# A convolution and expert kernel on one Trainium2 core: the second stage with batched scales, statistics collected for the choice, and square roots by Newton steps on VectorE

## The reference

```python
z = layernorm(_ln_c(x), ln_w, ln_b)
ab = sigmoid(z @ gate_w + gate_b) * (z @ lin_w + lin_b) * z_mask
g = sigmoid(z @ eg_w + eg_b)
B = einsum('bikc,bkjc->bijc', protein_pair, ab) + einsum('bikc,bjkc->bijc', ab, compound_pair)
x1 = x + g * (layernorm(B, lnc_w, lnc_b) @ as_w + as_b) * z_mask
t = _ln_t(x1)                      # 16384 tokens of 128
probs = softmax(t @ Wr + br)       # 8 experts, the best two, weights that sum to 1
h = gelu(layernorm(t) @ W1[e] + b1[e]);  y = h @ W2[e] + b2[e]
out = x1 + w_a * y_a + w_b * y_b
```

## Time and profile before

| | us |
|---|---|
| median of 3 runs (989.59 to 992.62) | 990.55 |
| the profiled execution | 992.77 |
| its span, first to last instruction | 990.9 |
| busy: TensorE | 752.3 |
| busy: VectorE | 634.3 |
| busy: ScalarE | 603.4 |
| busy: GpSimd | 583.5 |
| blocks of half 0 | 119 to 159 |
| second stage of half 0, first statistics to last x1 | 159 to 239 |
| choice of half 0 | 247 to 269 |
| second stage of half 1 | 304 to 404 |
| GpSimd's 128 row transfers | 269 to 487 |
| tiles of the experts | 493 to 991 |

### The profile page before, as it was taken

The page is one execution under the profiler, slowest core; times in us unless marked ns, Lnnn a source line. Parts: engine busy times, 40 slices in busy tenths (PEclk is TensorE's granted clock), DMA queues, the critical chain, the costliest instruction groups (busy, mean ns, idle before and its releaser), DMA issues.

```text
span 990.9 us, 24898 instructions
## 1 busy us (share of the span) xinstructions
PE 752.3 (76%) x7186; PEld 657.3 (66%) x7187; DVE 634.3 (64%) x2187; ACT 603.4 (61%) x1247; POOL 583.5 (59%) x547
## 2 busy tenths in 40 slices
PE   2788895667594674358098989989939989899893
PEld 1677794556493463312088879888938988898793
DVE  5766404996704898562187878878826767667572
ACT  1868895564594554401086768777817867777681
POOL 4545101543177886887545766767754767767674
PEclk9989997798797687755588999999989999999897
DMA  9993305474013246441133443434324434434420
GB/s 255 329 326 113 92 1 170 146 218 146 5 57 128 90 138 202 135 150 68 55 96 106 133 125 106 127 111 137 103 65 128 128 108 137 128 99 128 120 86 19
DMA packets 124019, 124.21 MB, mean 125 GB/s; under 512 B 21886, under 2 KB 91415, under 8 KB 123963
## 3 DMA queue, kind: packets, MB, share of 16 engines
q1 hardware_dynamic: 90212, 80.24, 28.5%
q0 software_dynamic: 15296, 34.64, 10.1%
q10 hardware_dynamic: 18456, 8.67, 3.1%
HBM read 77.21 MB, written 48.68 MB: 127 GB/s over the span
## 4 chain that ended last, share of the span: by engine, by line
PE 57%; POOL 14%; DVE 12%; issue 10%; ACT 3%; DMA 2%; SPq 1%; DVEq 0%; ACTq 0%; POOLq 0%
POOL row_dram L475 7%; PE ps L1219 6%; PE ps L1220 6%; PE ps L1221 6%; PE ps L1239 6%; PE ps L1242 6%; PE ps L1240 6%; PE ps L1081 6%; POOL row_dram L464 4%; PE ps L1198 4%; PE ps L1132 3%; POOL rs L454 2%; PE ps L1233 2%; DVE stats L888 1%; DVE work L949 1%
## 5 line engine op out<-in xcount | busy, mean ns | idle before, releaser
L1038 DVE TENSOR_TENSOR rows<-ABz,rows 128x512 f16<-128x512 f32 x280 | 193.9, 693 | 93.6 <-ACT rows L691 91.4
L513 POOL DMA_INDIRECT row_dram<-PPb x140 | 160.2, 1144 | 89.3 <-DVE PPb L1047 49.0
L516 POOL DMA_INDIRECT out<-PPb x140 | 160.6, 1147 | 84.6 <-DVE PPb L1047 45.3
L690 ACT ACTIVATE ABz<-ps 128x512 f32<-128x512 f32 x280 | 169.0, 603 | 54.5 <-PE ps L1221 46.4
L1239 PE MATMUL ps<-PPb,rows 128*128 x1120 | 187.9, 222 | 0.0
L1240 PE MATMUL ps<-PPb,rows 128*128 x1120 | 187.7, 221 | 0.0
L691 ACT ACTIVATE rows<-ps 128x512 f16<-128x512 f32 x280 | 170.0, 607 | 0.0
L1219 PE MATMUL ps<-B,PPb 128*128 128x256 f16 x560 | 157.2, 281 | 4.2 <-issue 4.2
L1220 PE MATMUL ps<-B,PPb 128*128 128x256 f16 x560 | 157.2, 281 | 0.0
L1221 PE MATMUL ps<-B,PPb 128*128 128x256 f16 x560 | 157.1, 281 | 0.0
L1242 PE MATMUL ps<-PPb,rows 128*128 x1120 | 155.7, 221 | 0.0
(11 more groups left out here) (233 smaller groups left out, 1549.7 us busy)
## 6 DMA issues: line engine op xcount, KB each, us to landing
PPb<-row_dram SPq DMA_DIRECT2D x70, 264.0 KB, 2.8
PPb<-in_L_conv_protein_pair SPq DMA_DIRECT2D x32, 512.0 KB, 6.2
PPb<-row_dram SPq DMA_DIRECT2D x70, 136.0 KB, 2.6
rows<-in_x SPq DMA_DIRECT2D x32, 256.0 KB, 6.3
g_dram<-work ACTq DMA_DIRECT2D x32, 256.0 KB, 2.4
work<-g_dram SPq DMA_DIRECT2D x32, 256.0 KB, 2.8
ABT<-in_x SPq DMA_DIRECT2D x32, 256.0 KB, 3.0
row_dram<-PPb POOLq DMA_INDIRECT x140
```

The lines of the kernel that those rows point to most:

```text
L513: pool.indirect_dma_start(row2_dram, bass.IndirectOffsetOnAxis(ap=Rw[:, u, b, POS:POS + 1].bitcast(u32), axis=0), Rw[:, u, b, :], None, bo ...
L516: pool.indirect_dma_start(out_rows, bass.IndirectOffsetOnAxis(ap=Rw[:, u, b, TOK:TOK + 1].bitcast(u32), axis=0), Rw[:, u, b, 0:D], None, b ...
L690: act.activation(Hf[:, u % 2, q, :], full, ACT.Gelu, scale=1.0 / SCALE)
L1038: dve.tensor_tensor(rest[:, part], Hf[:, u % 2, q, :], high[:, part], ALU.subtract).then_inc(h_parts[q], 1)
```

## The change

The second stage is written in another way; what is computed stays the same.

- The scales of B are made in two batches for a half, for columns 0 to 15 and for 16 to 63, by VectorE alone (`scale_b`): the reciprocal square root is a shift and a subtraction on the bits (`MAGIC`) and three Newton steps. ScalarE's `norm_b` reads them from one table, `bsc`.
- For x1, only the statistics are taken in a group's step; all that follows them is done in `choose`, for the whole batch, in 16 more links of its chain (`STATS`), with the same Newton steps.
- VectorE writes x1 straight to `rows`; ScalarE's copy L637 is gone, and the gate buffers are free once x1 is written. In half 1 the writing waits for `moved`.
- GpSimd has no power in this stage: it moves ten groups, sets some buffers, moves six more, and scatters.
- `ranks(0)` and `weights(0)` are moved behind the first blocks of half 1, which then no longer wait for the choice of half 0 but for the first link of it; `SPLIT` is 32.
- SyncE loads the experts' weights in the middle of half 1 instead of behind it. Four of eight folds on TensorE come before the tables' product.
- All loops of the stage are unrolled.

```diff
-SPLIT = 28
+HEAD = 4
+SPLIT = 32
 BATCHES = ((0, 0, NC), (1, 0, SPLIT), (1, SPLIT, NC))
-AHEAD = 7
+AHEAD = 10
+MAGIC = float(0x5F3759DF)
...
+        bsc = sb("bsc", [P, 2, NC])
...
+        STATS = 16
+        TAIL, FSTEPS = STATS + 23, 16
...
-                    wait_reuse(sp, s.x1_kept, n, 4, GH * h)
-                    wait_reuse(sp, s.x1T_psum, n, 4, GH * h)
+                    wait_reuse(sp, s.x1_done, n, 4, GH * h)
...
+                for n in range(GH):
+                    load_gates(n, n % 4)
                     if h == 0:
                         pp_piece(1, n)
-                pipeline(sp, GH, 4, [(0, load_gates), (0, next_half)], depth=4)
-            sp.dma_start(W1s, W1.rearrange("e d h -> d e h")).then_inc(fw_loaded, 16)
-            sp.dma_start(W2s, W2.rearrange("e (k p) d -> p e k d", p=P)).then_inc(fw_loaded, 16)
-            sp.dma_start(b1r, b1.rearrange("(o e) d -> o (e d)", o=1)).then_inc(fw_loaded, 16)
-            sp.dma_start(gbn[0:NE, :], ffn_g).then_inc(fw_loaded, 16)
-            sp.dma_start(gbn[NE:, :], ffn_b).then_inc(fw_loaded, 16)
-            sp.dma_start(b2s, b2.rearrange("(o e) d -> o (e d)", o=1)).then_inc(fw_loaded, 16)
+                    if h == 1 and n == GH // 2:
+                        sp.dma_start(W1s, W1.rearrange("e d h -> d e h")).then_inc(fw_loaded, 16)
...
-                    pipeline(pool, GH, 2, [((0, X1LAG), power)])
-                    pool.wait_ge(s.tail, 12)
+                    pool.wait_ge(s.tail, 1)
...
-                    for i in range(STEPS):
-                        power(i, i % 2, [i < GH, i >= X1LAG])
-                        if i % 2 == 0 and AHEAD + i // 2 < GH:
-                            move_rows(AHEAD + i // 2)
-                        if i == GH:
-                            pool.wait_ge(s.tail_done, 2)
-                        if i >= GH:
-                            scatter(TG * (i - GH), TG * (i - GH + 1))
-                    scatter(TG * X1LAG, SPLIT)
+                    for g in range(AHEAD, GH):
+                        move_rows(g)
+                    pool.wait_ge(s.tail_done, 2)
+                    scatter(0, SPLIT)
...
+                if h:
+                    act.wait_ge(s.tail, 1)
...
+                        if h and q == 10:
+                            weights(0)
...
+                def norm_b(n):
+                    act.wait_ge(s.b_ready, 2 * h + (1 if n < HEAD else 2))
+                    wait_reuse(act, s.bT_psum, n, 2, g0)
                     for t in range(TG):
-                        i = act.activation(zh[:, w, 0:2, :].rearrange("p a e -> p (a e)")[:, t * C:(t + 1) * C],
-                                           B[:, bass.ds(n * TG + t, 1), :].rearrange("p a c -> p (a c)"), ACT.Identity,
-                                           bias=shift2[:, w, t:t + 1], scale=rsm2[:, w, t:t + 1])
+                        j = n * TG + t
+                        i = act.activation(bh[:, n % 2, t * C:(t + 1) * C], B[:, j, :], ACT.Identity, bias=bsc[:, 1, j:j + 1], scale=bsc[:, 0, j:j + 1])
...
-                    act.activation(rows[:, bass.ds(n * TG, TG), 0:D], gr[:, u, :, :], ACT.Copy).then_inc(s.x1_kept, 1)
...
+                for t in range(GH + 6):
+                    if t < GH:
+                        norm_b(t)
+                    if 0 <= t - 1 < GH:
+                        bT_copy(t - 1)
+                    if 0 <= t - 4 < GH:
+                        x1T_copy(t - 4)
+                    if 0 <= t - 6:
+                        logit_copy(t - 6)
+                    if h and t == SPLIT // TG + 6:
+                        weights(1)
...
+                dve.wait_ge(s.x1_stat, GH * h + j1 // TG)
+                sc = c.stat[:, 0:3 * nj].rearrange("p (v j) -> p v j", v=3)
+                v, y, hv, sq = (c.stat[:, a * nj:(a + 2) * nj].rearrange("p (v j) -> p v j", v=2) for a in (3, 5, 7, 9))
+                st = x1st[:, j0:j1, :]
+                dve.tensor_tensor(sc[:, 0, :], st[:, :, 1], st[:, :, 4], ALU.add)
+                dve.tensor_tensor(sc[:, 1, :], st[:, :, 1], st[:, :, 4], ALU.subtract)
+                tail(dve.tensor_tensor(sc[:, 2, :], st[:, :, 2], st[:, :, 5], ALU.add))
+                dve.tensor_scalar(sc[:, 0, :], sc[:, 0, :], -0.5, None, ALU.mult)
+                tail(dve.tensor_tensor(sc[:, 1, :], sc[:, 1, :], sc[:, 1, :], ALU.mult))
+                tail(dve.scalar_tensor_tensor(sc[:, 2, :], sc[:, 1, :], D / 4.0, sc[:, 2, :], ALU.mult, ALU.add))
+                dve.tensor_scalar(v[:, 0, :], sc[:, 2, :], 1.0 / D, 1e-5, ALU.mult, ALU.add)
+                tail(dve.tensor_scalar(v[:, 1, :], sc[:, 2, :], (1.0 + 1e-5) / D, 1e-10, ALU.mult, ALU.add))
+                dve.tensor_scalar(hv, v, -0.5, None, ALU.mult)
+                tail(dve.tensor_scalar(y.bitcast(i32), v.bitcast(i32), 1, None, ALU.arith_shift_right))
+                tail(dve.tensor_scalar(y.bitcast(i32), y.bitcast(i32), -1.0, MAGIC, ALU.mult, ALU.add))
+                for _ in range(3):
+                    tail(dve.tensor_tensor(sq, y, y, ALU.mult))
+                    tail(dve.tensor_tensor(sq, sq, hv, ALU.mult))
+                    tail(dve.scalar_tensor_tensor(y, sq, 1.5, y, ALU.add, ALU.mult))
...
+                def scale_b(j0, j1, i):
+                    nj = j1 - j0
+                    st = bst[:, j0:j1, :]
+                    m1, m2, m4, y = (work[:, a:a + nj] for a in (896, 960, 1920, 1984))
+                    hv, sq = (work[:, a:a + nj] for a in (512, 560))
+                    mask = Mk[:, GH * TG * h + j0:GH * TG * h + j1]
+                    bstep(i)
+                    dve.tensor_tensor(m1, st[:, :, 1], st[:, :, 4], ALU.add)
+                    dve.tensor_tensor(m2, st[:, :, 1], st[:, :, 4], ALU.subtract)
+                    bstep(dve.tensor_tensor(m4, st[:, :, 2], st[:, :, 5], ALU.add))
+                    dve.tensor_scalar(m1, m1, -0.5, None, ALU.mult)
+                    bstep(dve.tensor_tensor(m2, m2, m2, ALU.mult))
+                    bstep(dve.scalar_tensor_tensor(m4, m2, C / 4.0, m4, ALU.mult, ALU.add))
+                    bstep(dve.tensor_scalar(m4, m4, 1.0 / C, 1e-5, ALU.mult, ALU.add))
+                    dve.tensor_scalar(hv, m4, -0.5, None, ALU.mult)
+                    bstep(dve.tensor_scalar(y.bitcast(i32), m4.bitcast(i32), 1, None, ALU.arith_shift_right))
+                    bstep(dve.tensor_scalar(y.bitcast(i32), y.bitcast(i32), -1.0, MAGIC, ALU.mult, ALU.add))
+                    for _ in range(3):
+                        bstep(dve.tensor_tensor(sq, y, y, ALU.mult))
+                        bstep(dve.tensor_tensor(sq, sq, hv, ALU.mult))
+                        bstep(dve.scalar_tensor_tensor(y, sq, 1.5, y, ALU.add, ALU.mult))
+                    bstep(dve.tensor_tensor(bsc[:, 0, j0:j1], y, mask, ALU.mult))
+                    bstep(dve.tensor_tensor(m1, m1, bsc[:, 0, j0:j1], ALU.mult))
+                    dve.tensor_tensor(bsc[:, 1, j0:j1], m1, mask, ALU.add).then_inc(s.b_ready, 1)
...
+                    if h:
+                        dve.wait_ge(moved[n % 4], (n // 4) * (16 * TG) + 16 * TG)
                     dve.wait_ge(s.as_mul, n + (1 + g0))
-                    dve.tensor_tensor(gr[:, u4, :, :], gr[:, u4, :, :], xk[:, u4, :, :], ALU.add).then_inc(s.x1_done, 1)
-                pipeline(dve, GH, 4, [(X1LAG, gate_b), ((0, X1LAG), statistics), ((1, X1LAG + 1), deviations)],
-                         after=(GH, lambda: choose(1)) if h else None)
+                    dve.tensor_tensor(rows[:, n * TG:(n + 1) * TG, 0:D], gr[:, n % 4, :, :], xk[:, n % 4, :, :], ALU.add).then_inc(s.x1_done, 1)
+                    dve.wait_ge(s.x1_done, n + (1 + g0))
+                    for t in range(TG):
+                        i = dve.bn_stats(x1st[:, n * TG + t, :], rows[:, n * TG + t, 0:D])
+                    i.then_inc(s.x1_stat, 1)
...
+                scale_b(0, HEAD * TG, stat_b(0, HEAD * TG))
+                stat_b(16, 32)
+                gate_b(0)
+                stat_b(32, 48)
+                gate_b(1)
+                scale_b(HEAD * TG, NC, stat_b(48, NC))
+                for n in range(2, GH):
+                    gate_b(n)
+                    if h and n == SPLIT // TG + 3:
+                        choose(1)
...
-                if h:
-                    ranks(0)
...
+                    if h and m == 1:
+                        ranks(0)
...
+                    if h and t == SPLIT // TG + 6:
+                        ranks(1)
...
+            pe.wait_ge(s.am_done, 1)
+            for e in range(4):
+                fold(e)
```

More of the change, by code:

```diff
@@ L669, in _ @@
                     a.then_inc(s.am_done, 1)
[L670 removed]
+                    weights(2)
             for e in range(NE):
@@ L811, in choose @@
+                sh, dv = (rows[:, j0:j1, q:q + 1].rearrange("p j o -> p (j o)") for q in (SH, RS))
+                dve.tensor_scalar(dv, y[:, 1, :], 1.0, None, ALU.mult)
+                tail(dve.tensor_tensor(sc[:, 0, :], sc[:, 0, :], y[:, 1, :], ALU.mult))
```

(3 more changed lines are left out.)

233 lines of the change are left out of this document (85 added, 148 removed).

## The result

The changed kernel takes 945.48 us (median of 4 runs, 940.19 to 949.20) where the kernel before takes 991.59 (989.59 to 994.27) on the same chip: ratio 0.953, with a 95% interval of 0.948 to 0.958. Run once more beside other kernels it took 946.27 (944.36 to 946.58), ratio 0.954 (0.951 to 0.957). The forecast was 941, and its rivals reached from under 928 to 995. The profiled execution has a span of 943.5 us where before had 990.9.

What follows compares the result with a forecast made beforehand. The bound was taken as a ladder to GpSimd's last row transfer: x1 and choice of half 0, half 1's blocks, part-stage and first choice, 81 us scatter. Its end moves from 487.3 to 437.8, 49.5 us sooner: 941 us, range 922 to 962.

Steps and rivals of the forecast that it cites:

- The start: Head of the second stage, counted from 159.3 us: gate 0 at 11.7 us, gate 1 at 16.4, gate 2 at 25.5.
- The cold steps: Early half 0, TensorE at low clock: 5.3 us a whole step, priced for three groups; gate 6 at 38.5 us.
- The step: Second stage: 2.6 us a step by the engines, TensorE longest at 2.64; in half 0 loads need 3.5 a group.
- Start of GpSimd: Half 0: last x1 at 222.3 us, choice's old part at 228.3, GpSimd's row transfers 21.9 later, at 250.
- Blocks of half 1: Transpositions and copies to 235 us, then blocks of 39.6 and 0.6 for two sigmoids: statistics at 275, instead of 303.9.
- The wait for the weights: Half 1: gates 9 to 15 queue behind the experts' weights on SyncE, costing VectorE 6.5 us ahead of gate 9.
- The scatter: GpSimd in half 1, from the first choice at 353: 81 us for 64 transfers plus 4 for one long, ending 437.8.
- Sum: Whole kernel: last transfer 49.5 us sooner, 437.8 for 487.3; profiled execution 943.3 us, 941 at the median's level.
- A: Rival in half 1: gates don't suffer from the weights' loading, 6.5 us less, 934.5 us; chance 0.2.
- B: Rival, second stage: steps near 4 us from engine waits and falling clock, or slower loads; 961 us; chance 0.15.
- D: Rival: TensorE stays at 1.2 GHz through both stages, every step 5.3 us; 995 us, slower; chance 0.03.
- C: Rival, GpSimd's scatter: transfers take 1144 instead of 958 ns, 12 us more, 953 us; chance 0.07.

## Why the prediction came out

The mechanism was right: the chain of the last transfers, its release by the first choice of half 1, GpSimd idle ahead of it (19.6 us, I had 20), folding over well before. The end of the scatter, 438.1, was forecast as 437.8. It is in part luck, since terms of several us cancel:

- **The start.** I counted from 159.3; the first scale's instruction starts at 157.97, 1.3 us sooner. The heads took what I said: gate 0 after 11.5 us (11.7), gate 2 after 24.9 (25.5), gate 3 at 186.86 (188.3).
- **The cold steps.** I priced the steps to the gates of groups 4 to 6 at or near the low clock, so that gate 6 would come 38.5 us after the start; it came after 36.0 (194.01), with steps of 2.3 to 2.5. The nine steps from there took 24.6 us where I had 23.4, since the loads slow the last four.
- **The step.** 2.6 was taken from TensorE's stretch in the earlier trace rows; the runs show 2.43, and by the rows it is TensorE that sets it, as forecast, with VectorE (2.22 to 2.30 alone) just behind. The 2.64 us in the earlier trace rows run to the modelled end of the last product; counted so the changed kernel's stretch is 2.58 (200.02 to 202.60), but the next step's first product starts before that end, at 202.44. The loads' step was 3.16, not 3.5: I took a share of 1.0 of the transfer engines as full, and it was 1.11. With the start, all this makes the last x1 220.0 instead of 222.3.
- **Start of GpSimd.** 246.8, forecast 250. The choice's old part (L816 of before, L821 now) starts at 227.23 for 228.3: of the 2.3 us won with x1 the new links gave back 1.2 (7.2 us from x1 for 6.0). From there it took 19.5 us and not the 21.9 that I took over: before had 2.31 us of waiting for the ranks in it, now 0.47 are left, though I had feared 2 or 3 more.
- **Blocks of half 1.** Statistics at 270.82, forecast 275: 2.3 us of x1, and 1.9 in the logits and transpositions ahead of the blocks, which start at 230.84 and not 235. The blocks themselves took 40.0 us, forecast 40.2.
- **The wait for the weights.** The term that was mis-sized most: 6.5 us forecast, 11.41 measured. More than all of the difference is that VectorE came sooner, with group 9 due at 314.3 (325.67 less 11.41) and not 321.5, 7 us sooner; the weights' issue took 15.9 us (304.88 to 320.79) for 14.5 in the earlier trace rows, and the gate starts 4.9 us after that, where I gave 3.4. Part of what was won ahead of such a date is paid back at it: the first choice came at 349.9 for 353.
- **The scatter.** 88.2 us for 64 transfers, forecast 84.8 (81 and 4 for one long one, taken over from the trace of before). Of the 3.4 us only 0.8 are in the long one, 5.8 for the 5.0 of before, whose cause, left unnamed, is VectorE's row of W2. Nearly all of the rest is in the other transfers, together 2.9 us over, which take up to 1.66 us each instead of 0.958; before had 2.4 of that kind, and my sum left them out.
- **Sum.** The choice forecast 3.1 us too late, the scatter 3.4 too short: 438.1 for 437.8. The tiles took 1.8 us more than the 503.6 that I took over. The profiled execution is so forecast as 943.3 and measured as 945.3; the rest of the distance between 941 and 945.5 is that before's profiled execution lay 2.2 us above its median and this one does not.

Of the rivals: A (no wait for weights) is refuted by the trace. Made true by moving the weights it gives 935.0; that this is close to the 934.5 of its price is chance, since the edit won 10 us and not 6.5, from 945.5 and not 941. B (steps near 4) did not come, but its mechanism exists: with ScalarE's copies taken at once steps take about 6.1 us at a mean clock of 0.79, and the whole is 1001.65, past B's price and D's 995. C needed transfers of 1144 ns; the median stayed 958; its mechanism, VectorE in GpSimd's way, is there, but costs 7.7 us in one row and some single instructions, most of which before paid too. D needed a clock of at most 0.55 over the stages; it was 0.69 in the head and 1.00 in the steps.

## What to carry to other kernels

In a loop that goes through several engines in a circle, ask of each in-order engine what stands behind each wait: taking two outputs one step later was worth 55 us in the changed kernel, part of it because TensorE kept its clock. Behind a change that makes a stage denser, look for the first fixed date, a bulk load in the same queue as the stage's own small ones; put it behind the last of them that is needed soon. And before trusting a total that fits, compare the marks along the chain: here two terms of 3 us had opposite signs. A last point is from the doubled statistics: an engine that is made longer and then sets the step need not have set it before; by how much less than the added work the step grew tells the room that it had.

## What the runs showed of the hardware

- Eight instructions of VectorE in a row, 128x512 fp32 to f16 with two inputs in SBUF (4.88 us), held one of GpSimd's indirect transfers for 5.0 to 5.8 us instead of 0.96, in every profile of a kernel that has the row; where both were read, the transfer ended 0.83 or 0.84 us after the row. One at a time they cost at most 0.24, by the same distance.
- SyncE took 10.2 to 13.5 us to issue a transfer of 16 KB behind 4 MB of weights, in the kernel before (388.10, 10.21 us) and in the nine others beside it, while in the changed kernel GpSimd's own transfers went on at 0.96 us each.
- TensorE's granted clock fell from 1.00 to 0.57 when steps of 4.25 us had gaps of about 2 us, and was 0.79 over 24 us of which it was busy 15.4; the kernel before, busy 14.5 of the same 24 us with steps of 4.66, had 0.91. In folds of which it was busy 32.66 of 40 us it had 0.50.
